# Gate and up products of 13 shared tiles inside the attention loop, and routing arithmetic of 14 tiles in the last attention steps

## The reference

```python
def _clamped_swiglu(x, wg, wu, wd):
    g = jnp.clip(x @ wg.T, -ALPHA, ALPHA)          # ALPHA = 7
    u = jnp.clip(x @ wu.T, -ALPHA, ALPHA)
    return jax.nn.silu(g) * u @ wd.T
...
logits = flat @ router_w.T
scores = jnp.sqrt(jax.nn.softplus(logits))
_, idx = jax.lax.top_k(scores + expert_bias, K)    # K = 4 of E = 32
topv = jnp.take_along_axis(scores, idx, axis=1)
topv = topv / (topv.sum(axis=-1, keepdims=True) + 1e-20)
...
out = out + _clamped_swiglu(flat, shared_gate_w, shared_up_w, shared_down_w)
...
x = x + _L0_xattn_ref(_layernorm(x), ctx_2048, ...)
x = x + _L0_ffn_ref(_layernorm(x), ...)
```

## Time and profile before

| | us |
|---|---|
| median of three runs | 1391.63 |
| lowest, highest | 1389.08, 1395.12 |
| the profiled execution | 1390.22 |
| its span | 1388.2 |
| attention loop, 256 steps | 164 to 821 |
| shared expert and routing | 821 to 949.5 |
| routed stage | 949.5 to 1388.2 |

### The profile page before, as it was taken

The page is one execution under the profiler, slowest core; times in us unless marked ns, Lnnn a source line. Parts: engine busy times, 40 slices in busy tenths (PEclk is TensorE's granted clock), DMA queues, the critical chain, the costliest instruction groups (busy, mean ns, idle before and its releaser), DMA issues. The chain is left out here.

```text
span 1388.2 us, 29575 instructions
## 1 busy us (share of the span) xinstructions
PE 1207.4 (87%) x7490; PEld 598.3 (43%) x7587; DVE 1104.9 (80%) x2279; ACT 937.6 (68%) x1339; POOL 876.1 (63%) x897
## 2 busy tenths in 40 slices
PE   7999577888887888887888787999999999999995
PEld 3444134444444444444444343444444444444442
DVE  4567899999999999999999955674676766667663
ACT  2235499999999999999999964224555555555552
POOL 3222388998989998989898871225544454445543
PEclk9999799999999999999999989999999999999998
DMA  7564977777667676766776886646678787787442
GB/s 260 142 155 116 174 128 137 143 137 147 139 136 145 139 147 133 151 140 132 141 146 125 145 180 220 160 122 159 154 195 227 231 240 172 183 243 186 86 69 27
DMA packets 398729, 215.54 MB, mean 155 GB/s; under 512 B 357063, under 2 KB 357191, under 8 KB 398674
## 3 DMA queue, kind: packets, MB, share of 16 engines
q1 hardware_dynamic: 378338, 176.05, 53.0%
q0 software_dynamic: 20336, 38.83, 15.7%
HBM read 100.84 MB, written 37.49 MB: 100 GB/s over the span
## 5 line engine op out<-in xcount | busy, mean ns | idle before, releaser
L548 ACT ACTIVATE mem<-mem 128x2048 uint8<-128x2048 f32 x256 | 534.3, 2088 | 45.7 <-POOL mem L664 41.0
L681 POOL TENSOR_SCALAR mem<-mem 128x2048 bf16<-128x2048 uint8 x256 | 485.7, 1898 | 27.9 <-DMA mem<-mem 7.8
L462 PE MATMUL psS<-mem 128*128 128x512 bf16 x929 | 293.3, 390 | 125.5 <-DVE mem L607 56.0
L607 DVE TENSOR_SCALAR_CACHE_REDUCE mem<-psS,mem 128x1024 f32<-128x1024 f32 x256 | 327.6, 1280 | 3.4 <-PE psS L462 3.4
L591 DVE TENSOR_SCALAR_CACHE_REDUCE mem<-psS 128x1024 f32<-128x1024 f32 x256 | 312.5, 1221 | 12.7 <-PE psS L462 10.4
L1328 PE MATMUL psS<-mem 128*128 x624 | 293.9, 594 | 0.5 <-issue 0.5
L1229 POOL DMA_INDIRECT out_y<-mem x78 | 123.9, 1588 | 189.9 <-DVE mem L1405 98.6
L861 DVE TENSOR_SCALAR mem<-psS 128x512 f32<-128x512 f32 x94 | 64.9, 691 | 162.4 <-PE psS L1328 121.3
L835 PE MATMUL psS<-mem 128*128 (+1 forms) x376 | 178.4, 597 | 1.5 <-ACT mem L849 1.5
L462 PEld LDWEIGHTS psS<-mem 128*128 128x128 bf16 x1024 | 68.1, 99 | 250.3 <-DVE mem L591 155.1
L480 PEld LDWEIGHTS psAV<-mem 128*128 128x128 bf16 x4096 | 138.8, 96 | 78.9 <-POOL mem L681 23.5
(11 more groups left out here) (221 smaller groups left out, 1326.1 us busy)
## 6 DMA issues: line engine op xcount, KB each, us to landing
mem<-in_moe_w SPq DMA_DIRECT2D x64, 768.0 KB, 6.4
mem<-xn_dram SPq DMA_DIRECT2D x32, 256.0 KB, 3.0
xn_dram<-mem SPq DMA_DIRECT2D x29, 256.0 KB, 2.1
mem<-in_x SPq DMA_DIRECT2D x28, 256.0 KB, 2.9
mem<-mem SPq DMA_TRANSPOSE x292, 3.1
mem<-in_ctx_in SPq DMA_DIRECT2D x16, 256.0 KB, 3.6
out_y<-mem SPq DMA_DIRECT2D x16, 256.0 KB, 2.2
mem<-in_wkv SPq DMA_DIRECT2D x2, 1024.0 KB, 7.1
```

The costliest lines, as they stand in the source:

```text
L462: last = nc.tensor.matmul(psS[c][:, k * D:(k + 1) * D], qT[pm][:, hm, :], kT[:, hm, c * HALF + k * D:c * HALF + (k + 1) * D], start=True, ...
L548: nc.scalar.activation(p8[slot], S[slot], ACT.Exp, bias=NB[:, slot:slot + 1], scale=sq[p][:, h:h + 1], accum_out=Z[p][:, h:h + 1]).then_in ...
L607: nc.vector.tensor_scalar(S[before][:, HALF:TK], psS[1][:], 1.0, M[:, 2 * before:2 * before + 1], ALU.mult, ALU.max, accum_out=M[:, 2 * be ...
L681: nc.gpsimd.tensor_scalar(pb[slot], pT[slot].bitcast(U8).rearrange("p (j q b) -> p j b q", b=2, q=P), 1.0, 0.0, ALU.mult, ALU.add).then_in ...
```

## The change

Tiles 0 to 12 of the shared expert (`GATED = 13`) get their gate and up products in the attention loop. In tile t, from 3 on, `pe_step` multiplies the transposed `xn2` of tile t - 3 with one 128-row piece of the gate and up weights in each of the steps h = 0 to 3, into the bank `psAV[p]` that is free until h = 7. ScalarE copies it into x1's buffer at h = 4, GpSimd clamps it there at h = 5, SyncE stores it to `gated_dram` at h = 6. The weights (1 MB in four transfers) are loaded at step 18. Behind the loop, `sp_early` loads these tiles back in the place of `xn2`; Silu and product read them there. Six hidden transposes and down products (`EARLY = 6`) stand in the steps l = 2 to 13 of the last pair. The routing arithmetic up to the masks is cut in two: 14 tiles (`TA`) in the steps l = 0, 3 and 7, the last two after the last logits. All lists come after the shared tiles that TensorE still makes in full, three of them. `pool_first` stands behind all 16 additions. The pair of tiles 2 and 3 is written out ahead of the loop.

```diff
+        def gated(t):
+
+            return not isinstance(t, int) or 3 <= t < TT
...
             if h == 14:
                 pe_route(pe, t - 2, 1)
+            if h < DC and gated(t):
+                if h == 0:
...
+                    pe.wait_ge(x1_ready, t - 1)
+                    pe.wait_ge(router_ev, t - 2)
+                last = nc.tensor.matmul(psAV[p][:], xn2T[:, h, :], gate_w[h], start=(h == 0), stop=(h == DC - 1))
+                if h == DC - 1:
+                    last.then_inc(early_mm, 1)
...
+            if h == 4 and gated(t):
+                act.wait_ge(early_mm, t - 2)
+                act.wait_ge(xn2_ready, t - 1)
+                act.wait_ge(x1_stored, 16 * (t - 1))
+                nc.scalar.activation(x1, psAV[p][:], ACT.Copy).then_inc(early_out, 1)
...
+            if h == 5 and gated(t):
+                pool.wait_ge(early_out, t - 2)
+                apart(pool, t)
+                nc.gpsimd.tensor_scalar(x1, x1, 7.0, -7.0, ALU.min, ALU.max).then_inc(early_clamped, 1)
...
+            if isinstance(n, int) and n == H + 2:
+                for c in range(DC):
+                    sp.dma_start(gate_w[c], moe_w[E, :, c * 2 * I:(c + 1) * 2 * I]).then_inc(gate_w_in, 16)
+            if h == 6 and gated(t):
+                sp.wait_ge(early_clamped, t - 2)
+                apart(sp, t)
+                sp.dma_start(rows(gated_dram, t - 3), x1).then_inc(early_stored, 16)
...
                 if l == 1:
-                    pe_tokens(pe, 0, 0)
-                if l == 2:
                     pe.wait_ge(shared_in, 16 * SHARED_PIECES)
...
+                if 2 <= l < 2 + 2 * EARLY:
+                    k = l // 2 - 1
+                    if l % 2 == 0:
+                        pe_hidden(pe, k, k % 2)
+                    else:
+                        pe_down(pe, k, k % 2, shared_weights)
+            pe.wait_ge(router_ev, TT)
+            pe.wait_ge(logits_cp, TT)
+            for k in range(EARLY, GATED):
+                pe_hidden(pe, k, k % 2)
+                if k > EARLY:
+                    pe_down(pe, k - 1, (k - 1) % 2, shared_weights)
+                if k == GATED - 4:
+                    pe_ranks(pe)
+            for k in range(GATED, SHARED):
                 o, before_o = k % 2, (k - 1) % 2
...
             for l in range(PAIR):
                 dve_step(dve, TT // 2, l)
                 if l == 0:
...
+                    hidden(0)
+                    hidden(1)
+                    soft_first(most, 1)
+                    hidden(2)
+                if l == 3:
+                    soft_last(most, 1)
+                    hidden(3)
+                if l == 7:
+                    choose_first(most, range(0, TA), 1)
+                    hidden(4)
+                    choose_last(most, range(0, TA), {1: 5})
...
-            for k in range(1, SHARED):
+            for k in range(2, SHARED):
                 add(k)
-                if k == SHARED - 4:
-                    pool_first(pool)
+            pool_first(pool)
```

381 lines of the change are left out of this document (199 added, 182 removed).

## The result

The changed kernel took **1404.8 us** (median of 4 runs, 1402.4 to 1406.7), the kernel before 1392.2: a ratio of 1.0098, with a 95% interval of 1.0076 to 1.0119. It is slower by about 1%, and the forecast of 1382 with a range of 1371 to 1397 was wrong. The profiled execution took 1406.7 us, its span is 1405.0.

A forecast was written before the change was run, and what follows sets the result against it. VectorE's maxima were taken to bound the loop, TensorE the shared stage. 1390.2 - 17.2 (earlier routed product) + 5.3 (loop) + 2.5 (low-clock restart) = 1380.8; with the median 1.4 above the profiled execution, 1382 us, range 1371 to 1397.

The forecast's parts named there:

- The loop: Attention loop: 13 tiles grow by 0.33 us each, plus 1 us for transposes delayed by the weights' load: +5.3 us.
- Step 1: End of attention: routing arithmetic and downs in the queues bring tile 15's x1 copy 15 us later, at 849.9.
- Step 2: From the last logits to the ranks: mask at 864.4 (before 870.9), ranks at 875.7 (before 877.90).
- Step 3: From the ranks through slots and lists to the rows: rows ready at 924.7, before 927.68.
- The slots: Right behind the ranks: slots take 9.4 us, before 14.2, and are ready at 885.1.
- The lists: From slots to rows: gate waits of 5.5, 1.6 and 1.9 us, four choices of names and places; rows at 924.7.
- Step 4: Start of the routed experts: first gather at 925.0, first routed product at 932.3, 17.2 us earlier; low-clock restart +2.5 us.
- D: Shared stage: gate and up products move but the routing chain isn't shortened at all; 1387 us, chance 0.10.
- A: End of attention: TensorE's low clock doubles 17 us of work on the chain; 1399 us, chance 0.15.
- B: Loop: GpSimd's lag isn't absorbed, a tile grows by 1.05 us, 13.7 instead of 4.3; 1391.6 us, chance 0.19.
- C: Shared stage: the walk is too pessimistic, tile 15 is 8 us late instead of 15; 1374 us, chance 0.18.
- The rule on table loads: ScalarE: each table switch adds a drain of about 1.38 us, eight on the chain 11 us; 1393 us, chance 0.02.

The follow-up runs named there:

- e13: e5 with GpSimd's clamp left out of the loop: 1381.2 us, 0.9929 of the kernel before.
- e12: e5 with ScalarE's copy of the gate and up products left out of the loop: 1382.6 us, 0.9940 of the kernel before.
- e6: e1 with only two shared tiles' transposes and downs in the last attention steps, behind the x1 copy, and the ranks behind tile 5's: 1392.2 us, 0.9996.
- e8: Changed kernel with the routing arithmetic of all 16 tiles behind the last logits: 1402.0 us, 1.0068 of the kernel before.
- e11: e5 with the routing arithmetic of all 16 tiles behind the last logits: 1392.9 us, 1.0026 of the kernel before.
- e1: Changed kernel with all SyncE loads of shared rows issued ahead of the expert weights: 1396.5 us, 1.0043 of the kernel before.
- e7: e1 plus TensorE products that nobody reads, only from tile 13's transposes on: 1391.2 us, 0.9999 of the kernel before.
- e5: e1 with tile 13's gate and up products ahead of tile 12's transposes, those of 14 and 15 ahead of tile 13's: 1386.0 us, 0.9956.
- e10: e5 and e6 orders together, gates and hidden products behind list names, last two lists ahead of tile 15's transposes, plus 13 fillers: 1379.3 us, 0.9914.
- e17: e10's orders and 13 fillers, first two shared tiles behind ScalarE's square of the last x1, first gathers ahead of tile 15's addition: 1371.6 us, 0.9864.
- e2: Changed kernel plus unread TensorE products wherever it waited, and a wait for 14 tiles' logits copies: 1405.1 us, 1.0117 of the kernel before.

## Why the prediction was wrong, step by step

**The loop** was nearly right: +5.8 for +5.3, with 5.6 to 8.4 in other executions. From 490.6 to 738.6 us the copies of x1 are 41.3 us apart, where they were 41.0 before: the 0.33 a tile of the forecast. Whether it is GpSimd's clamp that pays it, as the prediction said, isn't shown: without the clamp these tiles still take 41.2 (e13), without the copy or half of the products 41.3. GpSimd's waits for VectorE went from 5.1 us to 0.6. I had not seen one wait: TensorE's values product at step 7 waits for ScalarE's copy in every gated tile.

```profile
PE psAV L494 <- ACT mem L558: 18.7, 13, 2.5
```

No run shows that it costs anything: TensorE also waits 56 us for VectorE there, and e12, without the copy, was 0.8 us shorter. The third short wait of VectorE per tile did not show: in 200 to 800 us it waited 7.1 us for TensorE in 25 waits, before 8.3 us in 27. Three tiles at 322 to 449 us took 41.8 to 42.7 us; in e13 they took 41.1 to 41.8, and the rest of their cause stays open.

**Step 1**, tile 15, predicted at +15 us to the copy of x1, came at +16.6. The mechanism was named rightly: TensorE's queue, with downs between its last attention steps. e6 confirms it by taking them out: 13 us sooner. But the prediction called the delay the price of moving the routing arithmetic forward, and that is the smaller part: without the early arithmetic the copy came only 4.4 us (e8) and 6.9 us (e11) sooner, and at 29.7 in e8 still 12.2 us later than before.

From the copy to the logits it was 7.9 us for 7.0.

**Step 2**, the ranks, took 2.1 us more than walked, 0.8 of it up to the mask. The 2 us for the clock were a little too few: the row at 878.26 shows 1.7 on one down, and the next took 2.76 us for 1.88. The rest isn't traced to a cause.

**Step 3** is the step that failed, with 14.6 of the 22.4 us by which the first routed product came late. One term of it was missing, the wait for the rows, and one was too small, the waits for the gates.

- The slots (9.4 predicted, 14.1 measured). I took the durations and forgot the transfers: the new order asks for the rows of tiles 10 to 12 sooner than SyncE's queue delivers them behind 768 KB loads. I had written that each queue moved past matters, and had costed SyncE's only inside the loop. e1 gives it back: 9.3. The Trainium skill (DMA: Bandwidth & Descriptors, Queues, rings and completion order) says that each DMA engine takes a queue's descriptors in ring order. By that rule, the trace agrees: issued between the weights, the row loads landed after a median of 13.7 us, and all ahead of them after 4.1; the SiLUs waited 0.35, 2.04 and 4.04 us for them.
- The lists (39.6 predicted, 49.5 measured). The waits for the gates were seen, and seen to come from the order, but sized at 9.0 us for 17.0. Of the 8.0, 2.7 are at the first gate and come from the late rows as well: with the rows in time it waits 5.4 us (e1, e7, e8), against 5.5 forecast. The other two gates waited 8.7 us for 3.5. The prediction gave the low clock 2 us at the ranks and 2.5 at the restart, none in the lists, where TensorE is idle about half of the time: the stretch 920 to 964 has 0.69. One up of three took 4.43 us there for 3.60, the downs 3.7 to 3.8 for 1.88. At a clock of 1.00 (e7) the two gates waited 5.2 us, 3.6 less. VectorE also waited 2.6 and 1.7 us for list products of TensorE (L980), for which the walk's terms leave 1.7 us. Of e7's gain, 3.0 us lie in the lists; the other 2.8 are the restart, which the prediction had at 2.5. e5 prices the order at 10.5 us. This overlaps with the clock's price, since a product that isn't waited for may be slow.

**Step 4.** From the first gather to the first product it was 9.7 us, against 7.3 in the walk: the transposes started 6.9 us after the gather, the upper end of the earlier trace rows, and ran at the low clock. The restart cost the +2.5 foreseen (up 6.10 for 3.64).

The sum of the profiled executions closes: 3.7 at the start, 0.5 in the loop, 22.4 from the last exponential to the first routed product, less 0.4 in the routed stage and 0.3 around the span: 25.9, from 1380.8 to 1406.7. e1 and e5 together bring that product forward by 18.1 us. That isn't a share of the 22.4: e5 also takes away most of the 9.0 us of waits for the gates that the walk had counted on.

**The rivals.** D (the chain isn't shortened) was the nearest in mechanism, with a chance of 0.10: the rows came 16 us later than before, where it had priced a few. A (low clock, 0.15) was the nearest in the number, 1399, partly by luck: it had one of the causes, in the wrong place. The clock cost little in attention's end (downs of 2.96 and 2.86 us for 1.88) and more in the lists. B did not happen. C was the wrong way. None of the three signs of being wrong came either (the loop grew by under 10 us, the clock was 0.73 in attention's end, the first gather waited for the rows alone): all three looked away from step 3. The error behind them all: I took the delays beside the chain as small, since none showed before. There they had stood under TensorE's 112 busy us. Once TensorE was no longer the bound, each of them came out.

The rule on table loads did not apply: activations start at the end of each load in the new order too, as at 846.56.

```profile
846.56 1.28 ACT L1019 ACT_TABLE_LOAD   x1
847.85 0.58 ACT L1019 ACTIVATE mem<-mem 128x448 f32<-128x448 f32 x1
```

## What to carry to other kernels

When work is taken off the bounding engine, what was hidden under it must be walked again in full: each in-order queue (SyncE's and GpSimd's too), at the low clock where the engine will now idle. Hoisting arithmetic pays only as far as the next late thing; here 9 us at the mask gave nothing until the loads and three products were moved, and then 7. The order in the queues moved the changed kernel from 1.0098 to 0.9876 without any change of what is computed. The same orders were not tried on the kernel before, so no run shows how much of the 1.2% comes from the change itself.

## What the runs showed of the hardware

A VectorE operation with one input slows as well beside a GpSimd cast. In e6 three casts ran from 827.14 to 833.03, and an addition of a constant to 448 columns took 1.96 us; the changed kernel had it at 0.39 us once the casts were over. VectorE in e6, then in the changed kernel:

```profile
829.32 1.96 DVE L1066 TENSOR_SCALAR mem<-mem 128x448 f32<-128x448 f32 x1
831.32 2.19 DVE L1067 TENSOR_TENSOR mem<-mem 128x448 f32<-128x448 f32 x1
```

```profile
835.23 0.39 DVE L1066 TENSOR_SCALAR mem<-mem 128x448 f32<-128x448 f32 x1
835.66 0.63 DVE L1067 TENSOR_TENSOR mem<-mem 128x448 f32<-128x448 f32 x1
```

The Trainium skill (GPSIMD Engine Reference, Specifications) names two-port modes beside two SBUF inputs as what contends with GpSimd; I had weighed only the second. Whether this addition runs in a two-port mode, no run here shows.

Keeping TensorE's clock up with filler products paid only where they stood in no chain: 5.3 us in e7, nothing that can be told in e10 and e17, and in e2, where some stood among the last attention steps, no gain although the clock was up.
